# The first context of layer 1's cross attention, prepared inside the attention block ahead of it

## The reference

```python
x = _layernorm(x + _L1_attn_ref(x, L1_attn_in_proj_weight, ...), axis=-1)
x = _layernorm(x + _L1_xattn_ref(ctx_1024, x, mask_BxS2_bk0, ...), axis=-1)

def _L1_xattn_ref(x, latents, key_padding_mask, kv_gate, ...):
    x = layernorm(x, gamma_media, beta_media)            # x: the context, per batch 1601 rows x 256
    latents = layernorm(latents, gamma_lat, beta_lat)    # the 512 rows of the batch
    kv = jnp.concatenate((x, latents * kv_gate), axis=1) # 2113 keys
    q = (latents @ Wq).reshape(b, n, HEADS, DIM_HEAD)    # 8 heads of 64
    k = (kv @ Wk).reshape(b, f + n, HEADS, DIM_HEAD)
    v = (kv @ Wv).reshape(b, f + n, HEADS, DIM_HEAD)
    ...                                                  # masked softmax over the keys, weighted sum, @ Wout
```

## Time and profile before

| | us |
|---|---|
| median of 3 runs | 2319.09 (2316.57 to 2324.06) |
| profiled execution | 2316.37 |
| its span, first to last instruction | 2314.6 |
| PE busy | 2003.6 (87%) |
| DVE busy | 1533.4 (66%) |
| ACT busy | 1153.9 (50%) |
| POOL busy | 953.6 (41%) |
| last Q/K fill of layer 1's attention ends | 821.71 |
| its last instruction on DVE ends | 909.44 |
| first transposes of the cross attention | 929.84 |
| its first V product | 949.77 |

### The profile page before, as it was taken

How to read it: one execution, slowest core, us unless ns; L and a number is a source line. 1 busy time by engine, 2 the same in 40 slices (tenths; PEclk the granted TensorE clock), 3 DMA queues, 4 the chain that set the end, 5 groups by cost and what they waited for, 6 DMA issues and landing times. The chain is left out here.

```text
span 2314.6 us, 35756 instructions
## 1 busy us (share of the span) xinstructions
PE 2003.6 (87%) x12692; PEld 1393.6 (60%) x12692; DVE 1533.4 (66%) x2470; ACT 1153.9 (50%) x2213; POOL 953.6 (41%) x749
## 2 busy tenths in 40 slices
PE   7888858994988983889999999999999996799992
PEld 4565537992343443556666666565666664699992
DVE  5687864553978795588788768887787886222224
ACT  3332311102357544568776777677776772233332
POOL 2233222322222131066675756675566665222223
PEclk9999978997999996899999999999999998799996
DMA  4100017211000001000000000000000001621113
GB/s 154 39 30 14 25 69 277 102 33 59 1 0 1 0 1 65 29 1 1 29 1 1 10 6 25 1 10 1 1 1 1 10 1 65 236 83 38 38 33 118
DMA packets 36715, 93.30 MB, mean 40 GB/s; under 512 B 5415, under 2 KB 24379, under 8 KB 31934
## 3 DMA queue, kind: packets, MB, share of 16 engines
q1 hardware_dynamic: 30462, 74.72, 9.0%
q0 software_dynamic: 6080, 16.29, 2.1%
HBM read 76.56 MB, written 14.44 MB: 39 GB/s over the span
## 5 line engine op out<-in xcount | busy, mean ns | idle before, releaser
L1984 POOL TENSOR_TENSOR x_total<-x_total,x_pt 128x1024 f32<-128x1024 f32 x189 | 446.7, 2364 | 175.5 <-ACT x_pt L2070 158.0
L2091 ACT ACTIVATE x_pt<-PS,x_maskf 128x512 f32<-128x512 f32 x544 | 332.5, 689 | 168.0 <-PE PS L2394 166.0
L2190 DVE TENSOR_TENSOR PS<-x_pt,PS 128x512 f32<-128x512 f32 x480 | 333.4, 695 | 65.9 <-ACT x_pt L2091 28.6
L2208 DVE TENSOR_TENSOR x_pt<-x_pt,PS 128x1024 f32<-128x1024 f32 x320 | 320.3, 1052 | 0.7 <-PE PS L2412 0.7
L2394 PE MATMUL PS<-x_qs,x_ks 64*128 64x256 f32 x2176 | 281.9, 395 | 1.5 <-ACT x_pt L2091 1.5
L2371 PE MATMUL PS<-x_pt,x_vs 128*64 128x256 f32 x2108 | 262.9, 388 | 20.2 <-ACT x_pt L2070 10.7
L2070 ACT ACTIVATE x_pt<-x_pt 128x1536 f32<-128x1536 f32 (+1 forms) x160 | 266.5, 1667 | 12.3 <-DVE x_pt L2208 12.1
L1143 PEld LDWEIGHTS PS<-m_xT,m_own 128*128 128x128 f32 x1984 | 235.0, 195 | 7.0 <-DVE m_own L1219 2.9
L2394 PEld LDWEIGHTS PS<-x_qs,x_ks 64*128 64x128 f32 x2176 | 199.2, 188 | 65.1 <-issue 39.1
L1143 PE MATMUL PS<-m_xT,m_own 128*128 128x128 f32 x1984 | 235.9, 278 | 2.8 <-DVE m_own L1219 2.4
L2371 PEld LDWEIGHTS PS<-x_pt,x_vs 128*64 128x64 f32 x2108 | 141.9, 137 | 137.5 <-issue 63.8
(11 more groups left out here) (294 smaller groups left out, 2830.3 us busy)
## 6 DMA issues: line engine op xcount, KB each, us to landing
f_w<-in_L_ffn_w SPq DMA_DIRECT2D x32, 1024.0 KB
a_ctxT<-in_ctxT SPq DMA_DIRECT2D x8, 800.5 KB, 4.3
f_w<-ys SPq DMA_DIRECT2D x24, 256.0 KB, 5.2
x_cx<-in_ctx SPq DMA_DIRECT2D x4, 1536.0 KB
l_w<-in_L_attn_w SPq DMA_DIRECT2D x6, 512.0 KB
a_xT<-in_xT SPq DMA_DIRECT2D x4, 512.0 KB, 5.2
X<-in_x SPq DMA_DIRECT2D x1, 2048.0 KB, 11.2
xr<-a_xn SPq DMA_DIRECT2D x16, 128.0 KB, 1.7
```

What stands on the lines that cost most here:

```text
L1984: ins = nc.gpsimd.tensor_tensor(total2[:], first, tile[:, 2 * k + 2:2 * k + 4, :], ALU.add)
L2091: nc.scalar.activation(pt[:, s % 2, t, :].rearrange("p (h n) -> p h n", h=2), PS[:, first:first + 2, half], ACT.Identity, bias=maskf[:, b ...
L2190: ins = nc.vector.tensor_tensor(acc, tile, acc, ALU.max)
L2208: nc.vector.tensor_tensor(p_, p_, PS[:, MB, None, :].to_broadcast([P, at.stop - at.start, SPAN]), ALU.subtract).then_inc(lowered, 1)
```

## The change

The first batch's context is no longer loaded, counted and normalised at the start of the cross attention, but in the attention block. The room is l_w: once the last group's Q and K are made, the Q and K columns of both halves are not read again. Tiles 0 to 7 of the context go to l_w[:, 0, 0:2048], tiles 8 to 12 to l_w[:, 1, 0:1280]. l_w now lives until the cross attention ends, and x_wv, x_wo and x_most are placed in it too, instead of tensors of their own.

- SP, in the attention block: after l_wo it waits for the last Q/K fill and issues the context in three loads (`load_rows`).
- DVE: 13 BN_STATS and 13 BN_AGGR between the norm of group 2 and the residuals of group 3.
- POOL: four steps on 13 columns between `rstd` of group 2 and that of group 3.
- ACT: 13 tiles normalised in place, after its last copy.
- Cross attention: DVE and POOL treat only the four latent tiles of the first batch there; the mask as floats comes after them. PE makes the three K uses that need context alone before the latents' transposes. The one semaphore of the weights is split, so that each use waits for its own load, and SP's order becomes x_cols, x_wk, x_wq, mask, x_wv, x_wo, gate. Later contexts are loaded by three issues instead of two.

```diff
+def load_rows(eng, g, b, loaded):
+    S2, cx = g["S2"], g["x_cx"]
+    c = g["ctx"][b]
+    n = 2 * P1 // D
+    whole = S2 // P
+    eng.dma_start(cx[0], c[0:n * P, :].rearrange("(t p) d -> p t d", p=P)).then_inc(loaded, 16)
+    eng.dma_start(cx[1][:, 0:whole - n, :], c[n * P:whole * P, :].rearrange("(t p) d -> p t d", p=P)).then_inc(loaded, 16)
+    eng.dma_start(cx[1][0:S2 - whole * P, whole - n, :], c[whole * P:S2, :]).then_inc(loaded, 16)
...
         @block.sync
         def _(sp):
             sp.dma_start(wo[:], g["L1_attn_wo"]).then_inc(wo_loaded, 16)
+            sp.wait_ge(ring_done, (J - 1) * USES + QK)
+            load_rows(sp, g, 0, g["x_loaded_first"])
...
             rstd(pool, J - 2)
+            pool.wait_ge(c_stats, 1)
+            nc.gpsimd.tensor_scalar(cve[:], cmv[:, :, 1], LN_EPS, None, ALU.add).then_inc(c_ve, 1)
+            nc.gpsimd.tensor_scalar(cnmu[:], cmv[:, :, 0], -1.0, None, ALU.mult).then_inc(c_negated, 1)
+            pool.wait_ge(c_ve, 1)
+            nc.gpsimd.tensor_tensor(crs[:], cve[:], g["mhalf"][:].to_broadcast([P, CT]), ALU.pow).then_inc(c_rs, 1)
+            pool.wait_ge(c_rs, 1)
+            pool.wait_ge(c_negated, 1)
+            nc.gpsimd.tensor_tensor(cshift[:], cnmu[:], crs[:], ALU.mult).then_inc(c_shift, 1)
             rstd(pool, J - 1)
...
                 turned(J - 1, s)
+            act.wait_ge(c_shift, 1)
+            for i in range(CT):
+                x = context_tile(i)
+                nc.scalar.activation(x, x, ACT.Identity, bias=cshift[0:rows(i), i:i + 1], scale=crs[0:rows(i), i:i + 1])\
+                    .then_inc(g["x_normal_first"], 1)
...
             norm(last - 1, 0)
             norm(last - 1, 1)
+            dve.wait_ge(g["x_loaded_first"], 48)
+            dve.wait_ge(c_set, 1)
+            for i in range(CT):
+                nc.vector.bn_stats(cbn[0:rows(i), i, :], context_tile(i)).then_inc(c_counted, 1)
+            dve.wait_ge(c_counted, CT)
+            for i in range(CT):
+                ins = nc.vector.bn_aggr(cmv[0:rows(i), i, :], cbn[0:rows(i), i, :])
+            ins.then_inc(c_stats, 1)
...
                 if gi == 0:
-                    for i in range(len(CGROUPS)):
+                    for i in range(len(CGROUPS) - 1):
                         made += turns(0, i)
-                    made += [("q", 0, 0)] + [("K", 0, 0, c) for c in range(NG)]
+                    made += [("K", 0, 0, c) for c in range(PURE)] + turns(0, len(CGROUPS) - 1)
+                    made += [("q", 0, 0)] + [("K", 0, 0, c) for c in range(PURE, NG)]
...
-            load_context(0)
+            sp.dma_start(cols[:], g["L1_xattn_cols"]).then_inc(cols_loaded, 16)
+            sp.dma_start(wk[:], g["L1_xattn_Wk"]).then_inc(wk_loaded, 16)
+            sp.dma_start(wq[:], g["L1_xattn_Wq"]).then_inc(wq_loaded, 16)
             sp.dma_start(mask8[:], g["mask"]).then_inc(mask_loaded, 16)
-            for dst, src in ((cols, "L1_xattn_cols"), (wq, "L1_xattn_Wq"), (wk, "L1_xattn_Wk"),
-                             (wv, "L1_xattn_Wv"), (wo, "L1_xattn_Wout"), (wg, "L1_ffn_gate")):
-                sp.dma_start(dst[:], g[src]).then_inc(w_loaded, 16)
+            for dst, src in ((wv, "L1_xattn_Wv"), (wo, "L1_xattn_Wout"), (wg[:], "L1_ffn_gate")):
+                sp.dma_start(dst, g[src]).then_inc(w_loaded, 16)
...
-            act.wait_ge(w_loaded, 16 * 6)
-            act.wait_ge(mask_ready, 1)
+            act.wait_ge(cols_loaded, 16)
...
                 if kind == "N":
-                    pe.wait_ge(ln_ready, b * NS + (NS if group == "lat" else t0 + nt))
+                    if b == 0 and group == "ctx":
+                        pe.wait_ge(g["x_normal_first"], t0 + nt)
+                    else:
+                        pe.wait_ge(ln_ready, b * NS - CT + (NS if group == "lat" else t0 + nt))
...
-            pe.wait_ge(w_loaded, 16 * 6)
             pe.wait_ge(consts, 2)
             for s in SLOTS:
+                if s == 0:
+                    pe.wait_ge(w_loaded, 16 * 3)
```

More of the change, by code:

```diff
@@ L1377, in layer1_weights, with first_context @@
     g["l1_prepare"] = prepare
+def first_context(nc, ctx, g):
+    w = g["l1_w"]
+    half = 2 * P1
+    g["x_cx"] = [w[:, k, 0:half].rearrange("p (t d) -> p t d", d=D) for k in range(KD)]
+    g["x_wv"] = w[:, 0, half:half + KD * PX].rearrange("p (k n) -> p k n", k=KD)
+    at = (-(-g["S2"] // P) - half // D) * D
+    g["x_wo"] = w[:, 1, at:at + PAIRS_X * D].rearrange("p (k n) -> p k n", k=PAIRS_X)
+    g["x_most"] = w[:, 1, at + PAIRS_X * D:at + PAIRS_X * D + 512]
+    g["x_loaded_first"] = ctx.enter_context(nc.semaphore("x_loaded_first"))
+    g["x_normal_first"] = ctx.enter_context(nc.semaphore("x_normal_first"))
+def load_rows(eng, g, b, loaded):
[6 more added lines that the diff above has]
+    eng.dma_start(cx[1][0:S2 - whole * P, whole - n, :], c[whole * P:S2, :]).then_inc(loaded, 16)
 def layer1_attention(nc, top, g):
@@ L1442, in share, with context_tile, rows @@
             return sc[:, grp % 2, s, t, :, None].to_broadcast([P, H1, HD1])
+        def context_tile(i):
+            n = 2 * P1 // D
+            return g["x_cx"][i // n][0:P if i < CT - 1 else LAST, i % n, :]
+        def rows(i):
+            return P if i < CT - 1 else LAST
         def rstd(pool, grp):
@@ L1755, in layer1_cross @@
         PS, X, LG, ident, ones = g["PS"], g["X"], g["LG"], g["ident"], g["ones"]
-        wv = sb("wv", [P, KD, PX])
+        wv, wo, most = g["x_wv"], g["x_wo"], g["x_most"]
         wq = sb("wq", [P, KD, PX])
         wk = sb("wk", [P, KD, PX])
-        wo = sb("wo", [P, PAIRS_X, D])
         wg = sb("wg", [P, KD, E])
@@ L1803, in layer1_cross @@
         TURN_SLOT = 5
+        PURE = sum(e <= S2 // P for e in EDGES[1:])
         def unit(u):
@@ L1909, in source @@
                 np_ = P if i < CT - 1 else LAST
-                return cx[0:np_, i, :], cx[0:np_, i, :], np_
+                rows = context_tile(i)
+                return rows, rows, np_
             return X[:, b * J + i - CT, :], ln[:, i - CT, :], P
@@ L2225, in _ @@
             STATS = {at: range(at * NS // 14, (at + 1) * NS // 14) for at in range(14)}
-            for i in range(NS):
+            for i in range(CT, NS):
                 counted[0, i] = stats(0, i)
-            for i in range(NS):
+            for i in range(CT, NS):
                 aggregate(0, i, counted[0, i])
-            for i in range(NS):
+            for i in range(CT, NS):
                 normalise(0, i)
+            dve.wait_ge(mask_loaded, 16)
+            nc.vector.tensor_scalar(maskf[:], mask8[:], -1e30, None, ALU.mult).then_inc(mask_ready, 1)
             for s in SLOTS:
@@ L2313, in fill @@
                     _, b, p, c = use
-                    pe.wait_ge(gated, b + 1)
+                    if (b, p) == (0, 0):
+                        pe.wait_ge(wk_loaded, 16)
+                    if b >= 1 or c >= PURE:
+                        pe.wait_ge(gated, b + 1)
+                    else:
+                        released(pe, ("N", 0, c, KD - 1))
                     at = key_cols(c)
@@ L2559, in build @@
         with ExitStack() as early:
-            layer1_weights(nc, early, g)
-            experts0(nc, ctx, g)
-            layer1_attention(nc, ctx, g)
-        layer1_cross(nc, ctx, g)
+            with ExitStack() as middle:
+                layer1_weights(nc, early, middle, g)
+                experts0(nc, ctx, g)
+                first_context(nc, early, g)
+                layer1_attention(nc, ctx, g)
+            layer1_cross(nc, ctx, g)
         experts1(nc, ctx, g)
```

49 lines of the change are left out of this document (28 added, 21 removed).

## The result

| | before | changed |
|---|---|---|
| median, first comparison (4 runs each) | 2318.53 | 2292.93 (2291.02 to 2296.62) |
| median, second comparison (7 and 4 runs) | 2317.62 | 2292.47 (2292.05 to 2292.65) |
| profiled execution | 2316.37 | 2294.18 |
| its span | 2314.6 | 2292.4 |

The ratio is 0.9894 in both comparisons, with an interval of 0.9877 to 0.9911 in the first: some 25 us faster, 21 to 29 by the interval. The way and the cause of the seam's gain were right, the size was 4 to 5 us too small in the medians and 1.3 in the span.

A forecast was written before the change was run, and what follows sets the result against it. PE, busy 87% of the span, was taken as the bound, with time to win where it stops or runs slow. Saving 20.9 us takes the profiled 2316.37 to 2295.5; the median, 2.7 above, gives 2298.2 us, range 2293 to 2307.

The forecast's parts named there:

- the seam's gain: Between layer 1's attention and cross attention: PE no longer waits for the context, so the first V comes 20.9 us earlier.

The follow-up runs named there:

- all_wait_k_last: all_wait with all five K uses put behind q, as in the kernel before; 2302.10 us in one run, against 2317.52 for before on its chip.
- again: The changed kernel once more, no edit; median 2292.47 us, against 2317.62 for the kernel before on the same chip.
- k_last: The changed kernel with the first batch's old order: all transposes, q, then five K; median 2294.99 us, against 2317.62 for before.
- all_wait: The changed kernel, but PE and ACT wait for all weights before their first cross-attention work; median 2303.08 us, against 2317.62 for before.
- cols_last: The changed kernel, but SP issues x_cols last of its seven loads instead of first; median 2302.69 us, against 2315.18 for before.
- warm: The changed kernel plus 36 unused identity transposes on PE behind its last projection; median 2294.22 us, against 2315.18 for before.

## What to carry to other kernels

A hole at a seam between blocks can be won back as far as the work behind it fits into waits that exist earlier (19.5 of 24.5 us here; what is left is the block's own end); add up what each engine does in the tail, and look which of them then ends the block, for there a late load costs one for one. When a wait is removed, ask for each semaphore that was hidden behind it: here one wait for all weights would have taken back 9.5 of 21.4 us, and a load of 4.5 KB issued last 10.0. And where two traces are compared, split them at the seam, since 1000 us of cross attention, the same to the instruction, wandered by up to 7 us here; and the medians of kernels that should hardly differ gained anything from 21.0 to 25.6.

## What the runs showed that I had not expected

After a hole of 14 to 24 us PE's clock rose under the context's transposes (0.98 behind them in all_wait_k_last) and fell again for q (3.65, 3.56, 3.23 and 3.60 us in four traces); with three K products in front of it q was fast each time (1.95 and 1.96). After a hole of 5 us it didn't fall in either order (1.96), though PE had as little to do ahead of q.

Executions vary ahead of the seam as well: in the kernels with the same instructions there (changed, again, k_last, all_wait, cols_last, warm, all_wait_k_last) the last projection ended between 904.4 and 911.5 us.
